# Attention with mixed heads: a softmax maximum of its own for each half of the keys, and one copy for both banks of a turned chunk

## The reference, cut to what matters

```
q, k, v = split(x @ Wqkv.T + bqkv); q = rope(q); k = rope(k)
logits = einsum('bhid,bhjd->bhij', q, k) * 0.25
logits = einsum('bhij,gh->bgij', logits, Wpre)      # heads are mixed before the softmax
attn   = softmax(logits, axis=-1)
attn   = einsum('bhij,gh->bgij', attn, Wpost)       # and after it
out    = einsum('bhij,bhjd->bhid', attn, v)
x      = layernorm(x + out @ Wout.T + bout)
```

## Time and profile before

| | us |
|---|---|
| median of 3 runs | 9106.78 (9100.24 to 9108.23) |
| the profiled execution, its own time | 9105.46 |
| its span, first to last instruction | 9103.7 |
| PE busy | 8367.6 |
| DVE busy | 8179.9 |
| ACT busy | 7239.7 |
| POOL busy | 5882.0 |

### The profile page before, as it was taken

One profiled execution on the slowest core, in us unless ns is written; L12 is line 12 of the kernel. 1 busy time (PEld: TensorE's weight loads), 2 busy tenths in 40 slices (PEclk: granted clock), 3 DMA queues, 4 the chain that ended last, 5 costly groups with the idle time before them and its releaser, 6 DMA issues.

```text
span 9103.7 us, 399510 instructions
## 1 busy us (share of the span) xinstructions
PE 8367.6 (92%) x158060; PEld 4657.2 (51%) x158060; DVE 8179.9 (90%) x12269; ACT 7239.7 (80%) x13696; POOL 5882.0 (65%) x12005
## 2 busy tenths in 40 slices
PE   7999999997799999999779999999977999999997
PEld 3555555554455555555445555555544555555554
DVE  7999999996899999999689999999968999999996
ACT  5888888885588888888558888888845888888884
POOL 5666666663566676667356667666636666766663
PEclk9999999998899999999889999999989999999998
DMA  0000000002000000000100000000020000000002
GB/s 30 7 8 9 8 8 8 9 8 68 21 7 8 8 9 7 8 8 9 67 21 8 8 8 9 8 8 8 9 67 21 8 8 8 9 8 8 8 9 76
DMA packets 100978, 143.32 MB, mean 16 GB/s; under 512 B 8097, under 2 KB 90657, under 8 KB 96801
## 3 DMA queue, kind: packets, MB, share of 16 engines
q1 hardware_dynamic: 99104, 117.57, 3.9%
HBM read 75.60 MB, written 41.94 MB: 13 GB/s over the span
## 4 chain that ended last, share of the span: by engine, by line
DVE 43%; PE 32%; issue 19%; DVEq 2%; ACT 1%; SPq 1%; DMA 1%; POOL 0%; POOLq 0%; ACTq 0%
PE psS L1172 16%; DVE top L814 14%; DVE big L828 13%; DVE pl L854 9%; PE psP L1192 6%; PE psO L1207 6%; PE psM L1218 1%; DVE top L820 1%; ACT big L642 1%; DVE rr L846 1%; PE psS L1305 1%; PE psS L1147 1%; PE psS L1334 1%; DVEq L813 0%; DMA d_ct<-cT 0%
## 5 line engine op out<-in xcount | busy, mean ns | idle before, releaser
L828 DVE SCALAR_TENSOR_TENSOR big<-psP,big 128x512 f16<-128x512 f32 x4096 | 2608.7, 676 | 289.8 <-ACT big L642 280.7
L814 DVE TENSOR_REDUCE top<-psS 128x1 f32<-128x1024 f32 x2048 | 2482.5, 1212 | 224.1 <-PE psS L1172 223.7
L642 ACT ACTIVATE big<-psP 128x512 f16<-128x512 f32 x4096 | 2199.5, 589 | 581.9 <-PE psP L1192 576.0
L1172 PE MATMUL psS<-KH,AH 128*128 128x512 f16 x8192 | 2466.1, 383 | 81.8 <-POOL AL L440 80.0
L1172 PE MATMUL psS<-KH,AL 128*128 128x512 f16 x8192 | 2441.9, 380 | 0.0
L1172 PE MATMUL psS<-KL,AH 128*128 128x512 f16 x8192 | 2441.3, 380 | 0.0
L624 ACT ACTIVATE pr<-psS,nb 128x1024 f32<-128x1024 f32 x2048 | 2281.4, 1114 | 69.9 <-ACT nb L611 3.9
L652 ACT ACTIVATE ph<-pr 128x1024 f16<-128x1024 f32 x2048 | 2151.8, 1051 | 32.3
L1192 PEld LDWEIGHTS psP<-rh,ph 64*128 64x128 f16 x32768 | 1433.9, 95 | 1221.8 <-DVE big L828 1037.8
L1192 PE MATMUL psP<-rh,ph 64*128 64x64 f16 x32768 | 1682.6, 192 | 383.0 <-DVE big L828 345.6
L854 DVE TENSOR_TENSOR pl<-pr,ph 128x1024 f16<-128x1024 f32 (+1 forms) x2048 | 2024.3, 988 | 0.0
(11 more groups left out here) (138 smaller groups left out, 8004.7 us busy)
## 6 DMA issues: line engine op xcount, KB each, us to landing
ph<-in_xT SPq DMA_DIRECT2D x16, 512.0 KB, 4.4
xr<-in_x SPq DMA_DIRECT2D x64, 128.0 KB, 2.1
d_x<-x SPq DMA_DIRECT2D x64, 128.0 KB, 1.7
d_xn<-xn SPq DMA_DIRECT2D x64, 128.0 KB, 1.7
d_lg<-lg SPq DMA_DIRECT2D x64, 128.0 KB, 1.7
d_ct<-cT SPq DMA_DIRECT2D x64, 128.0 KB, 1.7
Q<-in_w SPq DMA_DIRECT2D x8, 1024.0 KB, 12.2
out<-V SPq DMA_DIRECT2D x16, 512.0 KB, 3.3
```

The costliest lines, as they stand in the source:

```text
L642: a.activation(PT[:, hf * JH:(hf + 1) * JH, :, 0, i0:i0 + HQ], psP[:, ih, :].rearrange("p (j g i) -> p j g i", j=JH, g=H), ACT.Copy, scale ...
L814: v.tensor_reduce(top[:, t % 2, h:h + 1], psS[:, 2 * h:2 * h + 2, :].rearrange("p c n -> p (c n)"), X, ALU.max).then_inc(s_mx, 1)
L828: v.scalar_tensor_tensor(out=PT[:, js, :, 1, i0:i0 + HQ], in0=psP[:, ih, :].rearrange("p (j g i) -> p j g i", j=JH, g=H), scalar=MDROP, in ...
L1172: mm = pe.matmul(psS[:, c, :], A_[:, k8, k, :], K_[:, k, c * CW:(c + 1) * CW], start=n == 0, stop=n == 5)
```

## The change

The second half of the keys gets a maximum of its own, as the first has. The row bound on DVE is gone. In its place POOL takes the smaller of the two negative biases (`lower_bound`, `nm`), ACT's factor becomes two columns (`ff`, one for each half) and waits for `nm`, POOL sums in two operations (`ws`, then `tot`), and `weights` makes both columns of `rr` from the reciprocal `rc`. On POOL, `mixq` now stands between the minimum and the sum. ACT copies both banks of psP by one operation of 1024 columns, whose input steps through four columns of one bank, then four of the other; DVE's `mixed_low` stays at four operations of 512 columns, each pair behind one copy.

```diff
-        top = sb("top", [P, 2, 3])
+        top = sb("top", [P, 2, 2])
...
-        f0 = sb("f0", [P, 2])
+        nm = sb("nm", [P, 2])
+        ff = sb("ff", [P, 2, 2])
+        ws = sb("ws", [P, 2, 2])
+        rc = sb("rc", [P, 2])
...
@@ GpSimd @@
+                def lower_bound(T, t):
+                    p = t % 2
+                    g.wait_ge(s_nb, T * 2 + 2 + 1)
+                    apart(g)
+                    g.tensor_scalar(nm[:, p:p + 1], nb[:, p, 0:1], nb[:, p, 1:2], None, ALU.min).then_inc(s_nm, 1)
                 def total(T, t):
                     p = t % 2
                     g.wait_ge(s_exp, T * 2 + 2 + 1)
                     g.wait_ge(s_f, T + 1 + 1)
-                    apart(g)
-                    g.tensor_scalar(tot[:, p:p + 1], sums[:, p, 0:1], f0[:, p:p + 1], sums[:, p, 1:2],
-                                    ALU.mult, ALU.add).then_inc(s_tot, 1)
-
-                def first_half(T, t):
+                    g.tensor_tensor(ws[:, p, :], sums[:, p, :], ff[:, p, :], ALU.mult).then_inc(s_ws, 1)
+                    g.wait_ge(s_ws, T + 1 + 1)
+                    g.tensor_tensor(tot[:, p:p + 1], ws[:, p, 0:1], ws[:, p, 1:2], ALU.add).then_inc(s_tot, 1)
+
+                def weights(T, t):
                     p = t % 2
                     g.wait_ge(s_rec, T + 1 + 1)
-                    g.tensor_tensor(rr[:, p, 0:1], rr[:, p, 1:2], f0[:, p:p + 1], ALU.mult).then_inc(s_r0, 1)
+                    g.tensor_tensor(rr[:, p, :], ff[:, p, :], rc[:, p:p + 1].broadcast_to([P, 2]), ALU.mult)\
+                     .then_inc(s_r0, 1)
...
                     if one:
-                        total(T - 1, t_1)
+                        lower_bound(T - 1, t_1)
                     if live:
                         mixq(it, t + LEAD, first and t + LEAD < TG)
+                    if one:
+                        total(T - 1, t_1)
                     roots(t, work, 0)
                     if one:
-                        first_half(T - 1, t_1)
+                        weights(T - 1, t_1)
                         post(T - 1, t_1)
@@ ScalarE @@
                 def bound(T, t, h):
                     p = t % 2
-                    m = 2 * h
-                    a.wait_ge(s_mx, T * 3 + 2 * h + 1 + 1)
-                    a.activation(nb[:, p, h:h + 1], top[:, p, m:m + 1], ACT.Copy, bias=LIFT * math.log(2.0),
+                    a.wait_ge(s_mx, T * 2 + h + 1 + 1)
+                    a.activation(nb[:, p, h:h + 1], top[:, p, h:h + 1], ACT.Copy, bias=LIFT * math.log(2.0),
                                  scale=-SSCALE).then_inc(s_nb, 1)
...
                 def factor(T, t, early):
                     p = t % 2
+                    a.wait_ge(s_nm, T + 1 + 1)
                     if not early:
                         a.wait_ge(s_r0, T - 2 + 1 + 1)
-                    a.activation(f0[:, p:p + 1], nb[:, p, 0:1], ACT.Exp, bias=nb[:, p, 1:2], scale=-1.0).then_inc(s_f, 1)
-
-                def mixed_high(T, t, c, Gd):
-                    hf, ih = c // 2, c % 2
+                    a.activation(ff[:, p, :], nb[:, p, :], ACT.Exp, bias=nm[:, p:p + 1], scale=-1.0).then_inc(s_f, 1)
+
+                def mixed_high(T, t, hf, Gd):
                     a.wait_ge(s_D, T * 2 + hf + 1 + 1)
                     if t % TG == 0:
                         a.wait_ge(s_F, Gd * NC + 2 * hf + 2)
-                    i0 = (t % TG) * QI + ih * HQ
-                    a.activation(PT[:, hf * JH:(hf + 1) * JH, :, 0, i0:i0 + HQ],
-                                 psP[:, ih, :].rearrange("p (j g i) -> p j g i", j=JH, g=H),
+                    i0 = (t % TG) * QI
+                    a.activation(PT[:, hf * JH:(hf + 1) * JH, :, 0, i0:i0 + QI]
+                                 .rearrange("p j g (h i) -> p (j g) h i", h=2),
+                                 psP[:, :, :].rearrange("p h (a i) -> p a h i", i=HQ),
                                  ACT.Copy, scale=MDROP).then_inc(s_mh, 1)
...
                     mixed(0)
-                    mixed(1)
...
-                    mixed(2)
-                    mixed(3)
+                    mixed(1)
@@ VectorE @@
-                def row_bound(T, t):
-                    v.wait_ge(s_mx, T * 3 + 2 + 1)
-                    v.tensor_tensor(top[:, t % 2, 2:3], top[:, t % 2, 0:1], top[:, t % 2, 1:2], ALU.max).then_inc(s_mx, 1)
-
                 def mixed_low(T, t, c):
-                    v.wait_ge(s_mh, T * NC + c + 1 + 1)
+                    v.wait_ge(s_mh, T * 2 + c // 2 + 1 + 1)
...
-                    v.reciprocal(rr[:, p, 1:2], tot[:, p:p + 1]).then_inc(s_rec, 1)
+                    v.reciprocal(rc[:, p:p + 1], tot[:, p:p + 1]).then_inc(s_rec, 1)
...
                     if live:
                         half_max(T, t, 1)
-                        row_bound(T, t)
```

More of the change, by code:

```diff
@@ L227, in seq_layer @@
         s_nb = sem("s_nb")
+        s_nm = sem("s_nm")
+        s_ws = sem("s_ws")
         s_f = sem("s_f")
@@ L268, in seq_layer @@
         s_out = sem("s_out")
-        FROM_ONE = [s_A, s_nb, s_f, s_tot, s_rec, s_r0, s_rp, s_rh, s_rl, s_pl, s_plg, s_D, s_F, s_y, s_mx, s_exp, s_ph,
+        FROM_ONE = [s_A, s_nb, s_nm, s_ws, s_f, s_tot, s_rec, s_r0, s_rp, s_rh, s_rl, s_pl, s_plg, s_D, s_F, s_y, s_mx, s_exp, s_ph,
                     s_mh, s_ml, s_oc, s_CTc, s_t1, s_xb, s_st, s_nw]
```

## The result

The changed kernel takes 9159.22 us in the median (9155.38 to 9174.9, four runs) beside 9105.41 of the kernel before (9100.24 to 9108.23, four runs on the same chip): a ratio of 1.0063, with a 95% interval of 1.0046 to 1.008. It is 54 us slower. The forecast was 8978. The profiled execution took 9174.9, with a span of 9173.1; it is the slowest of the four, 15.7 above their median.

The account below looks back on a forecast made before the run. PE waits for DVE, whose row bound stalls on POOL's SBUF lock: 372 us. With 2.4 + 0.8 + 0.6 = 3.8 us a pass left, 243 us, the gain is 129: 9105.5 - 129 = 8976.5, median 8978; range 8790 to 9180.

Parts of the forecast that it names:

- 372 us of PE's waits to win: All PE's waits for DVE's L828, with hidden matmul tails: the most a faster DVE could win, 5.8 us a pass.
- row work that doesn't fit: DVE and ACT row work beyond 0.2 of slack at t = 8, 12, 13, some 0.27 each: 0.8 us a pass.
- minimum, its wait, GpSimd's order, split sum: ACT's factor waits for POOL's late minimum: 1.65 at t = 6, 0.1 at 7, 0.65 at 11; 2.4 us a pass.
- the one copy (and 0.02 of stalls): Late copy 0.04 a slot, long L854 blocked by L427 0.02: ten plain slots at 0.06, 0.6 us a pass.
- It fits, with 0.2 to spare: Loop of PE's turn, the 1024-column copy and L828 takes 3.31 us against PE's half slot of 3.52.
- ACT's load of 6.83: ACT's work in a plain slot, 6.83 us against PE's 7.04, so 0.21 over.
- ten plain slots: PE's waits of 5.8 us a pass of 16 slots equal ten plain slots' worth, 0.58 us in each.
- The other six are bound by PE: Six of 16 slots are bound by PE: output matmuls at t = 2 and 10, and what follows them.
- rival 4: No change: the stall moves from L820 to L854 and L427, late factors give back the rest; 9105 us, chance 0.11.
- 1 (nearly all is won, 8824): ACT's factor hardly ever waits; 90 us of PE's waits left, 8824 us, chance 0.25.
- 2 (slower, by ACT's wait for the minimum, in plain slots): Long L854 gets the lock before the minimum, 0.33 in ten slots: 9317 us, in half of them 9211; chance 0.13.
- 3 (the read that jumps is slow): ACT's copy reading psP across two banks runs at half speed, 0.96 more a copy: 9829 us, chance 0.06.

Follow-up runs that it names:

- no_min_two: Kernel before with a maximum for each half but no minimum, sum in one operation, copies of 512 columns: 8859.36 us, ratio 0.9731.
- no_min_merged: Kernel before with a maximum for each half but no minimum, sum in one operation, one copy of 1024 columns: 8957.68 us, ratio 0.9839.
- two_copies: Changed kernel with ACT's copies of 512 columns back, one for each bank: 9055.57 us, ratio 0.9945 to the kernel before.
- wait_both: Kernel before, its copies of 512 kept, but DVE waits for both copies before either half: 9254.6 us, ratio 1.0166.
- merge_only: Kernel before with only the one copy of 1024 columns: 9248.95 us, ratio 1.0157.
- min_wait: min_idle with one line more: ACT's factor waits for the minimum, its value still unused: 9047.93 us, ratio 0.9937 to the kernel before.
- min_idle: no_min_two with POOL computing the minimum behind L497, unused and with nobody waiting: 8882.95 us, ratio 0.9751 to the kernel before.
- reduce_bound: Kernel before with DVE's row bound taken by a tensor_reduce over the two columns of top, one SBUF input for two: 8994.24 us, ratio 0.9878.

## Why the prediction was wrong

The sign was wrong; 9159 lies inside the range of 8790 to 9180, close to its end. Its sum was: 372 us of PE's waits to win, 3.8 us a pass left behind. Measured, all three terms were too small, and they were all of the error (the working is from medians; 64 passes):

| term, us a pass | predicted | measured | from |
|---|---|---|---|
| row work that doesn't fit, and all else without minimum or wide copy | 0.8 | 2.0 | (372 - 245) / 64, no_min_two |
| minimum, its wait, GpSimd's order, split sum | 2.4 | 3.1 | (9055.6 - 8859.4) / 64 |
| the one copy (and 0.02 of stalls) | 0.6 | 1.6 | (9159.2 - 9055.6) / 64 |

Together 6.7 for 3.8: 2.9 x 64 = 186 us, and 8978 + 186 = 9164.

**The copy is the step that turned the sign.** The prediction said "It fits, with 0.2 to spare", and took 0.04 a slot. Its arithmetic of one loop (turn, copy, L828, turn, 3.31 against 3.52) was right: at t = 3 of the changed kernel PE's turn starts at 1041.92, L836 at 1043.93, 2.01 later for the 1.98 forecast, and from L836 at 1040.59 to that turn are 1.33. But that loop is not where it hurt. It had the other numbers as well: L828, L854, L814, bound, exponentials, high parts, copy follow each other across DVE and ACT, once round for each slot. With the wide copy that ring is 1.20 + 1.14 + 1.24 + 0.24 + 1.23 + 0.97 + 1.03 = 7.05 (1.14 is the long L862 that meets no lock, from 1069.02 to L827 at 1070.16 in the changed kernel), as long as PE's 7.04; with copies of 512 it is 0.48 less, 6.57. So in plain slots the wide copy used up all of the ring's slack, and whatever else delays it counts in full. I compared ACT's load of 6.83 with 7.04 and called the difference slack, but an engine with slack still sits in a ring of two engines; the load bounds a slot from below, and the ring does too. One thing does in the changed kernel: the long L862 gives 1.43 in the place of 1.14, the stall by L432 that the prediction put at 0.02, and 7.05 + 0.29 is the 7.34 seen. In no_min_merged, where the sum is ahead of L427, t = 14, 15 and 0 are 7.06 in the mean, the bare ring; in two_copies the stalled ring would be 6.86, and the slots at t = 15 and 0 are 7.05, PE's.

The ring is only part of the price, though: of the 1.6 a pass, t = 14, 15 and 0 hold 0.35. I costed the copy in ten plain slots; the table shows it as dear elsewhere: two_copies to changed, 0.44 at t = 3, 0.42 at t = 9, 0.58 at t = 6, 0.48 at t = 11 (and 0.79 the other way at t = 7). "The other six are bound by PE" was not true of slot 3 once the copy came late. DVE and then PE of the changed kernel:

```profile
1036.46 1.29 DVE L836 SCALAR_TENSOR_TENSOR big<-psP,big 128x512 f16<-128x512 f32 x2 [1.73 <-ACT big L656]
```

```profile
1041.92 0.20 PE L1199 MATMUL psP<-rh,ph 64*128 64x64 f16 x2 [0.44 <-DVE big L836]
```

At t = 2 PE has the output matmuls, and DVE waits straight for the copy, which is whole only half a pair later. From 1036.46 DVE then has no idle time until PE's turn at 1041.92 has waited 0.44 for it; two_copies has no wait of PE in that place. So where DVE comes out of a wait for the copy into a stretch without slack, PE pays the half pair. I have followed that at t = 3 alone; for t = 6, 9 and 11 wait_both and merge_only show that the lateness is the cause, not its way. So the step that failed is the 0.6 for the copy, and its reason, that only PE's loop and ACT's load had to fit.

**The minimum was right in kind and place.** f idle at t = 6 and 11, released by the minimum, covered at t = 1, nothing in the slots of 1145 to 1156: all seen. Not forecast were four waits at t = 0, one at each batch's start, told below. Sizes: 1.65 at t = 6 against a mean wait of 1.56 in the changed kernel's records and 1.30 of slot in min_wait; 0.1 at t = 7 against 0.12 (but with copies of 512 it comes back: 0.88 in two_copies, and 0.68 of slot in min_wait); 0.65 at t = 11, taken between 0 and 1.3, against 1.16: the tie went to L854 in most passes. The wait alone cost 165 us against 154 forecast; the minimum's own operation, put at nothing, 24, which is hardly clear of the noise. At t = 10, where I had it covered, no wait of it was seen. The four at a batch's start are the longest. There the first minimum stands behind the weights of the first seven chunks, and f and then PE wait for it; ACT and PE of the changed kernel:

```profile
4687.43 0.29 ACT L648 ACTIVATE ff<-nb,nm 128x2 f32<-128x2 f32 x1 [7.35 <-POOL nm L510]
```

```profile
4690.06 1.03 PE L1179 MATMUL psS<-KH,AH 128*128 128x512 f16 x2 [7.16 <-ACT pr L638]
```

Such waits of PE for the exponentials are 27.1 us in the changed kernel and 27.3 in min_wait, 1.1 in the kernel before and 0.8 in min_idle. Most is caught up on behind them: from a batch's first exponentials to DVE's first L836 are 20.1 us in the mean where they were 17.3, some 11 us in four batches.

**Row work was too small**, for three reasons that PE's waits for DVE in no_min_two show when they are put to their slots (worked out from its 314 waits, 134.8 us, 2.1 a pass; the 2.0 of the table comes from the times).

First, 34.5 us of them, 0.54 a pass, stand at the ends of the four batches, 16 waits of 1.9 to 2.8 us at the last turns, with few or no scores between them. The kernel before has 35.4 us there. So of the 372 us some 35 had nothing to do with the row bound, and leaving it out didn't win them; the prediction counted them among the slots of a pass.

Second, it had the wrong slots. It named t = 8, 12 and 13 at 0.27 each. The waits stand behind t = 5 (0.29), t = 8 (0.56) and t = 13 (0.72), and none at t = 12: that slot is 8.10 for the 7.3 it was to fall to because PE has the logits matmuls in it, and DVE idles. From PE's turn to that of the next slot, t = 12 is 7.87 in the kernel before and in no_min_two alike. PE and DVE of no_min_two at t = 12:

```profile
1078.41 1.03 PE L1225 MATMUL psM<-mu_s,xuT 128*128 128x256 f32 x4
```

```profile
1080.92 1.29 DVE L822 SCALAR_TENSOR_TENSOR big<-psP,big 128x512 f16<-128x512 f32 x2 [1.08 <-ACT big L641]
```

Third, the lock moved to the row work at t = 13 and 5. With no bound on DVE, other operations now stand where GpSimd has the port. In DVE's groups of before and of the changed kernel (the running column maximum):

```profile
L961 DVE TENSOR_TENSOR colmax<-colmax,lg 128x256 f32<-128x256 f32 x64 | 26.4, 412 | 0.0
```

```profile
L969 DVE TENSOR_TENSOR colmax<-colmax,lg 128x256 f32<-128x256 f32 x64 | 74.6, 1166 | 0.0
L862 DVE TENSOR_TENSOR pl<-pr,ph 128x1024 f16<-128x1024 f32 (+1 forms) x2048 | 2180.5, 1065 | 2.4 <-ACT ph L667 2.4
```

In no_min_two the maximum has 1167 as well, and it and a stalled long L848 fill t = 13, where DVE has no idle time at all:

```profile
1088.10 1.26 DVE L955 TENSOR_TENSOR colmax<-colmax,lg 128x256 f32<-128x256 f32 x1
1090.48 1.42 DVE L848 TENSOR_TENSOR pl<-pr,ph 128x1024 f16<-128x1024 f32 x1
```

So t = 13, which was to fall to some 7.3, stayed at 8.11. At t = 5 it is an integer shift of two columns, a tensor_scalar with one SBUF input, in before and then in no_min_two:

```profile
L897 DVE TENSOR_SCALAR ir<-vr x64: 154/155/170, 275.9 to 9010.0; 128x2 int32<-128x2 int32 x64
L891 DVE TENSOR_SCALAR ir<-vr x64: 169/1001/1004, 266.8 to 8760.5; 128x2 int32<-128x2 int32 x64
```

L862 grew from 988 ns in the mean (L854) to 1065, 2024.3 us in all to 2180.5. This was rival 4's stall that moves, seen in part; I had given it its own chance and no term in the forecast. I haven't removed it from the row work by itself, so its share of the 1.2 is argued, not measured.

**The rivals.** 1 (nearly all is won, 8824): false here, but the waits that it denied, with the copy, keep the changed kernel from it; no_min_two at 8859 is near it, with another factor and other copies. 2 (slower, by ACT's wait for the minimum, in plain slots): the sign came true and the mechanism didn't; in the plain slot of 1149.98 the factors follow the accumulator with no wait. 3 (the read that jumps is slow): refuted, 1.011 us. 4: above.

**What was to show it.** Held: no one-column operation near 1 us on DVE in plain slots (one of two columns with row work, L905, takes 998 ns in the median at t = 5); the copy near 1.05; f idle at t = 6 and 11. Failed: PE's waits, 385.0 for about 220. "L828 of half B within 0.6 of L814's end" held, with L827 ending at 1148.27 and L836 starting at 1148.79, and told nothing: those 0.52 were the ring.

## What to carry to other kernels

A step that gets longer but keeps its engine's load can still set the pace: follow the work round, across engines, from each operation back to its own next instance, and compare every such ring with the bound, not only the loads and the loop through the busiest engine. The plain slots of this case show it; in other slots the same lateness cost more than the ring says. A wide operation costs latency, and one that reads half its input late makes the next engine wait for the whole: before joining two, ask who starts on the first. And when a stall on a shared port is taken away, look which operations come next in that place. Here the row bound's own stall went at no cost by reducing over its two adjacent columns, but behind it two operations a pass took one up.

## What the runs showed that I had not expected

One ScalarE copy of 1024 columns from PSUM, read in runs of four columns across two banks, takes 1.011 us in the median and the next operation starts 0.90 after it (from 1155.10 to 1156.00), less than the 0.96 of a pair of 512: the jumping costs nothing that shows, ACT does save 0.06 a copy (for 2048 of them an estimated 120 us), where the prediction had nothing saved, and the kernel is 104 us slower for it.

The order of two operations on GpSimd is worth 67 us one way without the minimum's wait, and 24, near the noise, the other way with it.

Both attempts to take the row bound's stall away, by leaving it out (no_min_two) and by giving it one input (reduce_bound), made another VectorE operation take over 1 us in its place, once at t = 5 and once at t = 13 in the one, at t = 8 and 14 in the other.
